# Attention pooling over 2048 x 200 keys: keys of a tile in four transfers without waits between them, and another order at the front

## The reference

```
feat = concatenate([q, k, q - k, q * k])        # 512 per key
h = feat @ W1 + b1                              # 64 per key
h = where(h >= 0, h, alpha * h)
a = where(mask == 0, -1e9, h @ W2 + b2)         # one score per key
out = softmax(a over the 200 keys) @ k          # 128 per query
```

## Time and profile before

| | |
|---|---|
| median of 3 runs | 1019.24 us (1017.79 to 1035.44) |
| profiled execution | 1018.95 us, span 1017.0 us |
| busy | PE 83%, DVE 76%, POOL 65%, ACT 52% of the span |
| DMA | 222.45 MB, mean 219 GB/s; queue 1 65% of 16 engines |
| mean granted clock of PE | 0.983 |
| transpose of 6 rows by DVE (L340) | 0.97 us |
| step of the loop, from a tile's first transpose to the next's | 5.9 to 10.9 us |

### The profile page before, as it was taken

The page is one execution under the profiler, slowest core; times in us unless marked ns, Lnnn a source line. Parts: engine busy times, 40 slices in busy tenths (PEclk is TensorE's granted clock), DMA queues, the critical chain, the costliest instruction groups (busy, mean ns, idle before and its releaser), DMA issues.

```text
span 1017.0 us, 55327 instructions
## 1 busy us (share of the span) xinstructions
PE 847.9 (83%) x25216; PEld 559.4 (55%) x25216; DVE 769.4 (76%) x1143; ACT 532.8 (52%) x1281; POOL 656.3 (65%) x401
## 2 busy tenths in 40 slices
PE   0769888988888898889889889888887888888896
PEld 0435555655555565556555556555555555545564
DVE  2879777878788778787787888777886777867771
ACT  0355545655555565555555555555554555545552
POOL 0657666767667676676666667667666667657661
PEclk9899999999999999999998999999999999989999
DMA  8844766667776766786675777766677676667630
GB/s 253 322 148 138 268 204 212 233 201 239 253 236 228 238 206 230 238 270 211 229 231 185 236 266 238 232 223 226 204 242 257 211 230 209 217 225 233 213 103 11
DMA packets 67017, 222.45 MB, mean 219 GB/s; under 512 B 25312, under 2 KB 33504, under 8 KB 66784
## 3 DMA queue, kind: packets, MB, share of 16 engines
q1 hardware_dynamic: 66784, 218.92, 65.0%
HBM read 214.57 MB, written 4.33 MB: 215 GB/s over the span
## 4 chain that ended last, share of the span: by engine, by line
PE 40%; DVE 16%; DMA 15%; issue 13%; ACT 8%; SPq 7%; POOL 0%; DVEq 0%; ACTq 0%; POOLq 0%
PE hP L431 22%; DMA keys<-in_r_k 9%; PE poolP L472 9%; DVE act L348 9%; PE scoreP L460 7%; ACT act L289 6%; DVE keysT L340 5%; DMA probs_scratch<-expd 5%; SPq L160 3%; SPq L211 2%; ACT expd L313 2%; PE poolP L480 1%; DVE neg_max L361 1%; DVE logits L355 1%; DMA w2c<-in_L_rec_W 1%
## 5 line engine op out<-in xcount | busy, mean ns | idle before, releaser
L289 ACT ACTIVATE act<-hP,biast,al 128x200 f32<-128x200 f32 x1024 | 459.5, 515 | 329.6 <-PE hP L431 325.9
L340 DVE STREAM_TRANSPOSE keysT<-keys 128x768 f32<-128x768 f32 (+1 forms) x512 | 510.1, 997 | 60.4 <-DMA keys<-in_r_k 60.3
L431 PE MATMUL hP<-keysT,weff 32*64 32x200 f32 x16384 | 475.5, 344 | 30.3 <-issue 23.5
L232 POOL TENSOR_TENSOR weff<-qX,wp 128x1024 f32<-128x1024 f32 x128 | 244.0, 1906 | 324.3 <-PE hP L431 300.7
L431 PEld LDWEIGHTS hP<-keysT,weff 32*64 32x64 f32 x16384 | 310.2, 133 | 186.2 <-issue 113.1
L348 DVE TENSOR_TENSOR act<-hP,act 128x400 f32<-128x400 f32 x512 | 283.9, 554 | 146.8 <-ACT act L289 143.0
L236 POOL TENSOR_TENSOR weff<-weff,wk 128x1024 f32<-128x1024 f32 x128 | 303.2, 2369 | 10.0
L472 PE MATMUL poolP<-keys,pool_w 128*16 128x128 f32 x6400 | 244.6, 276 | 22.7 <-issue 21.2
L472 PEld LDWEIGHTS poolP<-keys,pool_w 128*16 128x16 f32 x6400 | 173.4, 97 | 98.1 <-issue 93.0
L460 PE MATMUL scoreP<-act,w2win 128*16 128x200 f32 x2048 | 151.3, 341 | 81.3 <-DVE act L348 70.3
L271 POOL TENSOR_TENSOR pool_w<-probs_k,own_b 128x400 f32<-128x400 f32 x128 | 111.3, 870 | 15.7 <-DMA probs_k<-probs_scratch 7.9
(11 more groups left out here) (35 smaller groups left out, 40.9 us busy)
## 6 DMA issues: line engine op xcount, KB each, us to landing
keys<-in_r_k SPq DMA_DIRECT2D x128, 832.0 KB, 5.5
keys<-in_r_k SPq DMA_DIRECT2D x128, 768.0 KB, 5.2
probs_scratch<-expd SPq DMA_DIRECT2D x32, 100.0 KB, 3.7
masks<-in_r_mask SPq DMA_DIRECT2D x128, 12.5 KB
probs_k<-probs_scratch SPq DMA_DIRECT2D x128, 12.5 KB
out_rows<-pooled SPq DMA_DIRECT2D x128, 8.0 KB
keys<-in_r_q SPq DMA_DIRECT2D x4, 256.0 KB, 5.0
act<-in_L_rec_W SPq DMA_DIRECT2D x4, 128.0 KB, 6.1
```

Of the source, the lines that this page charges most:

```text
L232: g_.tensor_tensor(weff[:, n % 2, :, :, :], qX[:, n, :, :].unsqueeze(3).broadcast_to([P, BQ, CD, H]), wp[:].unsqueeze(1).broadcast_to([P, ...
L289: a_.activation(act[:, k, a, :], hP[:, 2 * (p % HSETS) + a % 2, 0:L], ACT.Identity, bias=biast[:, n, k, a:a + 1], scale=al[:]).then_inc(t_ ...
L340: v_.transpose(keysT[:, n % TBUF, j0 * D:j1 * D], keys[:, n % SLOTS, j0 * D:j1 * D]).then_inc(keysT_done, 1)
L431: mm = t_.matmul(hP[H * r:H * r + H, 2 * (p % HSETS) + a % 2, 0:L], weff[QP * a:QP * a + QP, n % 2, w, c, :], kT[QP * a:QP * a + QP, :, c, ...
```

## The change

The keys of a tile are issued as four transfers with the pieces' borders (6, 6, 6 and 7 rows of each partition, 384 or 448 KB), right after each other. The waits for `keysT_done` in the loop and for the landing of tile n-2 at the front go; the wait for a free slot stays. Masks therefore follow the whole tile. At the front SP issues the parameters first. DVE transposes q before it folds; half of tile 0 is transposed beside the bias matmuls and half behind the bias; `nshift` precedes tile 1. PE and ACT wait for fold 11 later, and PE waits for `consts_done` only in `add_parts`.

```diff
--- before.py
+++ after.py
@@ -32,8 +32,6 @@
 TBUF = 3
 CUTS = [0, 6, 12, 18, J]
 PIECES = len(CUTS) - 1
-LOADS = 2
-LOAD_CUT = [0, 12, J]
 HEAD_J = 12
 HSETS = 3
 NEG = -1000000000.0
@@ -147,19 +145,22 @@
 
         @block.sync
         def _(sp):
-            def load_part(n, x):
-                at = slice(LOAD_CUT[x] * D, LOAD_CUT[x + 1] * D)
-                sp.dma_start(keys[:, n % SLOTS, at], k_tiles[n][:, at]).then_inc(keys_in[n % SLOTS], 16)
-
             def load_keys(n):
-                for x in range(LOADS):
-                    load_part(n, x)
+
+                for x in range(PIECES):
+                    at = slice(CUTS[x] * D, CUTS[x + 1] * D)
+                    sp.dma_start(keys[:, n % SLOTS, at], k_tiles[n][:, at]).then_inc(keys_in[n % SLOTS], 16)
 
             def load_mask(g):
                 for c in range(QUADS):
                     sp.dma_start(masks[QP * c:QP * c + HALF_Q, g % 2, :],
                                  mask_rows[g, c]).then_inc(mask_in[g % 2], 16)
 
+            sp.dma_start(al[:], alpha.rearrange("(a b) -> a b", b=1).broadcast_to([P, 1])).then_inc(params_in, 16)
+            sp.dma_start(b2c[:], b2.rearrange("(a b) -> a b", b=1).broadcast_to([P, 1])).then_inc(params_in, 16)
+            for r in range(2):
+                sp.dma_start(b1c[H * r:H * r + H, :], b1.rearrange("(a b) -> a b", b=1)).then_inc(params_in, 16)
+                sp.dma_start(w2c[H * r:H * r + H, :], W2).then_inc(params_in, 16)
             for a in range(QUADS):
                 sp.dma_start(q_sb[QP * a:QP * a + QP, :].rearrange("y (t e) -> y t e", e=BQ * D),
                              q_rows[a]).then_inc(q_in, 16)
@@ -167,14 +168,7 @@
                 sp.dma_start(w1[QP * a:QP * a + QP].rearrange("x f c h -> x (f c) h"),
                              w1_rows).then_inc(w1_in, 16)
             load_keys(0)
-            sp.dma_start(al[:], alpha.rearrange("(a b) -> a b", b=1).broadcast_to([P, 1])).then_inc(params_in, 16)
-            sp.dma_start(b2c[:], b2.rearrange("(a b) -> a b", b=1).broadcast_to([P, 1])).then_inc(params_in, 16)
-            for r in range(2):
-                sp.dma_start(b1c[H * r:H * r + H, :], b1.rearrange("(a b) -> a b", b=1)).then_inc(params_in, 16)
-                sp.dma_start(w2c[H * r:H * r + H, :], W2).then_inc(params_in, 16)
             for n in range(1, SLOTS):
-                if n > 2:
-                    sp.wait_ge(keys_in[n - 2], 16 * LOADS)
                 if n == 3:
                     sp.wait_ge(zeroed, 1)
                     load_mask(0)
@@ -184,23 +178,14 @@
                 load_keys(n)
 
             for n in range(STEPS):
-
-                def paced_part(x):
-                    if SLOTS <= n + AHEAD < TILES:
-                        behind = PIECES * (n + 1) + 2 + x * PIECES // LOADS
-                        sp.wait_ge(keysT_done, min(behind, PIECES * TILES))
-                        load_part(n + AHEAD, x)
-
                 if SLOTS <= n + AHEAD < TILES:
 
                     sp.wait_ge(part_done, n + AHEAD - SLOTS + 1)
-                paced_part(0)
+                    load_keys(n + AHEAD)
                 g = n // GT - 1
                 if n % GT == 1 and 0 <= g < GROUPS - 2:
                     sp.wait_ge(scores_read, g + 1)
                     load_mask(g + 2)
-                for x in range(1, LOADS // 2 + 1):
-                    paced_part(x)
                 if n % GT == 0 and 0 <= g < GROUPS:
                     sp.wait_ge(exp_done, g + 1)
 
@@ -210,8 +195,6 @@
                     for t in range(GT):
                         sp.dma_start(probs_k[:, g % 2, t, :], probs_tiles[g % 2, t]
                                      ).then_inc(probs_in[GT * (g % 2) + t], 16)
-                for x in range(LOADS // 2 + 1, LOADS):
-                    paced_part(x)
                 m = n - 1 - LAG
                 if m % GT == GT - 1 and 0 <= m < TILES:
                     g = m // GT
@@ -294,8 +277,7 @@
                 a_.activation(logits[:], neg[:], ACT.Identity, bias=nshift[:, g:g + 1]).then_inc(logits_ready, 1)
 
             a_.preload_act_table(ACT.Exp)
-            act_e.wait_ge(fold, 11)
-            fill(0)
+            act_e.wait_ge(bias_done, QUADS + 1)
 
             for n in range(STEPS):
                 m = n - 1 - LAG
@@ -305,6 +287,9 @@
                     a_.activation(parts[:, m % GT, :], poolP[:, 0:D], ACT.Copy).then_inc(parts_done, 1)
                 scale_pair(PAIRS * n - 1)
                 scale_pair(PAIRS * n)
+                if n == 0:
+                    act_e.wait_ge(fold, 11)
+                    fill(0)
                 g = n // GT - 1
                 if n % GT == 0 and 0 <= g < GROUPS:
                     act_e.wait_ge(max_done, g + 1)
@@ -334,7 +319,7 @@
                 if n >= TILES:
                     return
                 if piece == 0:
-                    dve.wait_ge(keys_in[n % SLOTS], (n // SLOTS + 1) * 16 * LOADS)
+                    dve.wait_ge(keys_in[n % SLOTS], (n // SLOTS + 1) * 16 * PIECES)
                     ge(dve, main_done, PAIRS * (n + 1 - TBUF))
                 j0, j1 = CUTS[piece:piece + 2]
                 v_.transpose(keysT[:, n % TBUF, j0 * D:j1 * D], keys[:, n % SLOTS, j0 * D:j1 * D]).then_inc(keysT_done, 1)
@@ -365,6 +350,8 @@
             v_.memset(poolP[:], 0.0)
             v_.memset(w2win[:], 0.0).then_inc(zeroed, 1)
             v_.memset(neg[:], NEG).then_inc(zeroed, 1)
+            dve.wait_ge(q_in, 16 * QUADS)
+            v_.transpose(qX[:].rearrange("p (t y) w c -> p t (w c) y", y=QP), q_sb).then_inc(qx_done, 1)
             dve.wait_ge(w1_in, 16 * QUADS)
             dve.wait_ge(params_in, 6 * 16)
 
@@ -377,10 +364,6 @@
             v_.tensor_scalar(wk[:], wk[:], sgn[:], None, ALU.mult).then_inc(fold, 1)
             v_.tensor_scalar(wp[:], w1[:, 3, :, :], sgn[:], None, ALU.mult).then_inc(fold, 1)
             v_.tensor_scalar(wq[:], wq[:], sgn[:], None, ALU.mult).then_inc(fold, 1)
-            dve.wait_ge(q_in, 16 * QUADS)
-            v_.transpose(qX[:].rearrange("p (t y) w c -> p t (w c) y", y=QP), q_sb).then_inc(qx_done, 1)
-            for piece in range(QUADS):
-                transpose_piece(0, piece)
             v_.tensor_scalar(b1s[:], b1c[:], sgn[:], None, ALU.mult).then_inc(fold, 1)
             v_.tensor_scalar(al1[:], al[:], 1.0, None, ALU.subtract).then_inc(fold, 1)
             dve.wait_ge(zeroed, 2)
@@ -388,6 +371,8 @@
                 mm = v_.tensor_scalar(w2win[H * r:H * r + H, HALF_Q - 2 + r:HALF_Q - 1 + r], w2c[H * r:H * r + H, :],
                                       sgn[H * r:H * r + H, :], None, ALU.mult)
             mm.then_inc(fold, 1)
+            for piece in range(2):
+                transpose_piece(0, piece)
             dve.wait_ge(bias_mm, 1)
             dve.wait_ge(fold, 9)
             for a in range(QUADS):
@@ -395,10 +380,12 @@
                                  b1s[:], None, ALU.add).then_inc(bias_done, 1)
             dve.wait_ge(bias_done, QUADS)
             v_.tensor_scalar(biast[:], bias[:], al1[:], None, ALU.mult).then_inc(bias_done, 1)
+            for piece in range(2, 4):
+                transpose_piece(0, piece)
+            dve.wait_ge(shift_mm, 1)
+            v_.tensor_scalar(nshift[:], scoreP[:, 0:GROUPS], b2c[:], -1.0, ALU.add, ALU.mult).then_inc(fold, 1)
             for piece in range(2):
                 transpose_piece(1, piece)
-            dve.wait_ge(shift_mm, 1)
-            v_.tensor_scalar(nshift[:], scoreP[:, 0:GROUPS], b2c[:], -1.0, ALU.add, ALU.mult).then_inc(fold, 1)
 
             for n in range(STEPS):
                 g = n // GT - 1
@@ -453,6 +440,8 @@
 
             def second_layer(n, k):
                 pe.wait_ge(act_done, PAIRS * n + 2 * k + 2)
+                if n == 0 and k == 0:
+                    pe.wait_ge(fold, 11)
                 if n % GT == 0 and k == 0:
                     ge(pe, scores_read, n // GT)
                 t = HALVES * (n % GT) + k
@@ -475,6 +464,7 @@
                     mm.then_inc(part_done, 1)
 
             def add_parts(g):
+                pe.wait_ge(consts_done, GT)
                 pe.wait_ge(parts_done, GT * (g + 1))
                 for t in range(GT):
                     mm = t_.matmul(poolP[:, D:2 * D], place[:, t, :], parts[:, t, :], start=(t == 0),
@@ -503,9 +493,6 @@
                                        w2win[:, HALF_Q - 2 - 2 * t:2 * HALF_Q - 2 - 2 * t], by_group[:, s, k, a, :],
                                        start=(t == 0), stop=(t == HALVES * GT - 1))
             mm.then_inc(shift_mm, 1)
-            pe.wait_ge(fold, 11)
-            pe.wait_ge(consts_done, GT)
-
             for n in range(STEPS):
                 m = n - LAG
                 late = n > LAG and m % GT == 0
```

## The result

| | before | change |
|---|---|---|
| median | 1018.51 us | 1058.45 us |
| ratio | | 1.041, interval 1.028 to 1.053 |
| profiled execution (span) | 1018.95 (1017.0) | 1071.90 (1070.2) |

The measured time lies above the whole range of the prediction (940 to 1000 us).

What follows compares the result with a forecast made beforehand. No engine was full; the chain (40% PE, 16% DVE, 15% DMA) was held by late keys after each softmax and instruction fetches. From 1018.95 us, -6 - 32 - 10 - 5 = -53 gave 966 us, 80% range 940 to 1000.

Steps and rivals of the forecast that it cites:

- Keys' wait: DVE's wait for the tile loaded after a group's softmax, 60.3 us, would nearly vanish: 32 us gained, bounds 17 and 36.
- the fit: Least squares over 28 group periods: 27.6 us + 0.59 x keys' wait + 0.71 x PE's mid-run idle + 0.41 x half clock.
- Front: At the kernel's start, parameters first would bring the first layer to 28.0 from 33.88 us: 6 us gained, bounds 8 and 4.
- Instruction fetch: PE's idle inside runs, waiting for instruction packets, would shrink with halved key transfers: 10 us gained, a third of the 29 possible.
- the packet near 35: Early instruction fetch, started at 35.0 us with key transfers still pending; read as waiting for one or two transfers, not all.
- The -25 us: Alternative size for the instruction-fetch term: engines alternate queues packet by packet, so the hold is halved outright.
- Half clock: PE's stretches at 1.2 instead of 2.4 GHz cost 10 us; half would go with the waits: 5 us gained, bounds 0 and 10.
- Twice the transfers: Two more issues per tile, 256 in all, some 100 us of SP's time, would cost nothing because SP waits longer anyway.
- starved instructions: Rival, 10%: instruction fetches wait out whole key bursts, up to 7.5 us, so PE idles; 1009 to 1079 us, middle 1044.
- rival of unchanged landings: Rival, 6%: keys after the softmax still land 7.5 us after first issue, a residue of 1.1 us a group; 996 us.
- pay-back: Rival, 12%: DVE catches up after its waits for keys, so only 0.28 of each wait is gained; 998 us.
- sign of being wrong: Wrong if keys' wait goes but periods stay at 30 us, or "issue" grows before first-layer and pooling matmuls.

Runs made afterwards that it cites:

- e1: The change with two transfers of 12 and 13 rows per tile instead of four, still without waits between them; 1.058 of the kernel before.
- e6: e1 with the loop's two waits per tile for DVE's transposes put back (new front, masks behind, two paced halves); 0.982 of the kernel before.
- e8: e1 with each transfer from tile 10 on bringing 6 rows in place of 12 or 13, about half of the bytes; 0.909 of the kernel before.
- e11: The change's four transfers per tile, released in pairs at the two points where the kernel before released its halves; 0.999 of the kernel before.
- e12: e6 run once more, on the same chip as e11; 0.979 of the kernel before.
- e2: The change with one transfer of 1600 KB per tile and no waits; 1.052 of the kernel before.
- e9: e6 with probabilities read back behind the next step's keys, whose parts go two transposes earlier; 0.976 of the kernel before.
- e5: The kernel before with one edit: after a softmax, the second part of the keys is issued before the four mask transfers; 0.988 of the kernel before.
- e10: e1 with the second half issued only when the first has landed, from tile 10 on, and no wait for DVE; 1.141 of the kernel before.

## Why the prediction was wrong, by its steps

- **Keys' wait (forecast -32 us)**: right in place and, by the fit, nearly in size. 47.6 of 60.3 us went, times 0.59 is 28. The chain lost its DMA share.
- **Front (-6 us)**: the first layer came 7.9 us earlier; parameters ahead of q cost it 3.5 us (SP's issues), the lower bound. Right.
- **Instruction fetch (-10 us)**: the step that failed, with its sign. PE's idle in runs went from 1.47 to 3.77 us a group; at the fit's 0.71 that is +46 us over 28 groups. The argument was that the packet near 35 had passed queued transfers, so the hold was a number of transfers and would halve with their size. Only its first half holds. At the front, where keys flow all the time, the first five fetches waited 2.8, 2.1, 2.7, 5.3 and 2.9 us before the change and 3.2, 3.7, 2.9, 2.4 and 2.8 after it: some 3 us, whatever the transfers' size. In the loop the old pauses had kept most fetches below that: of 198, 58 waited more than 2 us before the change and 86 after it, 89 in e1, 54 in e6 and 6 in e8. (When PE asks is not in the trace; it is taken near the end of each block of 256 of its instructions. Other places in the block give 41 against 77 or 86 against 119.)

  The Trainium skill (page "DMA: Bandwidth & Descriptors", section "Queues, rings and completion order") has engines alternate between queues by packets of 9 to 17 descriptors. The -25 us that I read out of it did not come. Between a request and its fetch up to 28 pieces of keys per engine passed in the change (3072 or 3584 bytes each) against 17 before (6144 or 6656 bytes): more pieces, and about as many bytes, 1.5 MB against 1.75.
- **Half clock (-5 us)**: followed the idle. 96 us against 37; in the 28 groups 2.68 us each against 0.85, at 0.41 another +21. (The row of 40 slices shows an 8 in only two slices between the first and the last group; the six stretches are in the trace, not in that row.)
- **Twice the transfers (0)**: nothing speaks against it in bursts (the change 1.041, e1 1.058). With pauses the quarters cost 2% against halves (e11, e12), which the prediction had no term for.
- **Left over** are 0.6 us a group, 17 us, by which the change's trace is slower than the fit. That this execution was above its median is not the reason: e1 and e2, traced near theirs, leave 0.9 to 1.0 us a group, and the kernel before and e6 leave none. So the fit prices starved kernels too low. Why is not shown; one way is that the kernel before often had another wait in which a stop of PE could hide. PE's own rows need no fit: per group its idle inside runs rose by 2.3 us, its busy time by 0.9, and its waits for other engines fell by 1.1, together 2.0, as the periods did (30.24 to 32.26).

The sum by measured terms: -8 - 28 + 46 + 21 + 17 = +48, against +53 between the traces. The missing 5 us lie outside the 28 groups: of the 8 us at the front 6.3 are left when group 3 begins, and the stretch behind the last group takes 3.2 us more. The rival that came true, starved instructions, had been priced at 1009 to 1079 with 1044 in the middle; it had 10%, and should have had more, since the trace of before already showed an idle of 0.93 us behind 3.3 us of keys, and the change made such stretches the rule. Its waits of up to 7.5 us did not come, though; the longest are some 5 us, before and after. The rival of unchanged landings is out, since the wait fell to 12.7 us. That of pay-back is not decided; e9 gained 6 us where the fit gives 16, and the fit's 0.59 has an error nearer 0.14 than 0.11. The sign of being wrong that the prediction had named, "issue" growing in front of the first layer and of pooling, is the one that came.

## What to carry to other kernels

A wait that looks idle on the issuing queue may be what lets another queue through. Before taking it out, look for PE's "issue" idle inside runs of equal matmuls and for the instruction packets beside it; if there are some, the pauses between large transfers can be worth more than the issue order (here 7% against 1%). Move small transfers off the critical place instead: masks behind the keys gave 1% with the waits in place (e5), and 2% together with the new front (e6). And a pause must not be a wait for the transfer's own landing, if its queue has other work.

## What the runs showed of the hardware

- A late instruction packet was held by key traffic for some 3 us, and at most for about 5. Without pauses that made some 120 us of PE's idle, however the traffic was cut (e1, e2, the change); with half of the bytes the idle was 7 us.

  The Trainium skill (page "Runtime: NRT & Kernel Launch", section "Instruction fetch mechanics") calls the cost of crossing a block mostly hidden. With the DMA engines 41% busy (e8, idle of 7 us) the runs agree; at 63% in bursts (the change, 117 us) they do not.
- PE went on 2.2 to 2.5 us (at most 2.9) after the start of a late instruction packet, whose own transfer took about 1 us.
- Half clock went with PE's idle of either kind. 22 of the change's 24 stretches at 1.2 GHz began within 8 us of a stop of 1 us or more. There were 37 us of it before, 96 in the change (117 us idle inside runs), and 189 in e10, where PE stood in 97 pieces for 206 us before the scores:

```profile
PE scoreP L456 <- DVE act L340: 206.2, 97, 6.7
```
